# Recurrent block of a four-layer kernel: the h=1 scan level as a token-pair sum on VectorE, and four mixes at once on four row groups

## Chip, cores and metric

The kernel runs on one core of a Trainium2 chip. The metric is device time in microseconds (us), the median of three runs. All data are float32.

## What is computed

The input x is 32 sequences (B) of 128 tokens (T) with D = 512. Four layers follow each other: attention over a context (layer 0), a non-local block (layer 1), a recurrent block of the RWKV kind (layer 2), and cross-attention with a perceptron (layer 3). The change lies in layer 2. There NH = 32 heads of HD = 16 columns are scanned:

```
xa  = layer_norm(x);  sx = previous token of xa - xa
xxx = tanh((xa + sx * maa_x) @ maa_w1)             # five groups of 32 columns
xm_j = xa + sx * (maa_stack_j + xxx_j @ maa_w2_j)  # five mixes: k, w, v, r, g
w = exp(-exp(time_decay + tanh(xw @ td_w1) @ td_w2))
r, k, v = xr @ Wr.T, xk @ Wk.T, xv @ Wv.T;  g = silu(xg @ Wg.T)
for each token t:                                  # state s: 16 x 16 for each head
    a   = k_t (outer) v_t
    out = r_t . (u * a + s)
    s   = a + w_t * s
x1 = x + (group_norm(out) * g) @ Wo.T
x2 = x1 + sigmoid(xr2 @ Wfr.T) * (relu(xk2 @ Wfk.T)**2 @ Wfv.T)
```

## The kernel before

The program has stages: phase_a (layers 0 and 1), phase_norm, phase_b (layer 2) and phase_c (layer 3). phase_b begins at about 1050 us and ends at about 2900 us. It takes the sequences two at a time (G = 2), so there are N = 16 pairs, and a loop of turns (function `run`). The order of work is written out by hand. `SLOTS_OF` (L756) has 18 rows. In row n every engine does scan step n of the current pair and then the steps of the other stages that the row lists: kind "p" (projections of the next pair), "l" (late projections of the current pair), "f" and "e" (what follows the scan, for the pair before and the one before that). Each engine walks the same table in its own program; semaphores tie them. An engine does its own instructions strictly in this order, so an instruction that waits holds all behind it.

**The scan** has for each of the two sequences nine steps: seven levels h = 1, 2, 4, ..., 64, then PRODUCT and TURNED. At level h the tokens are cut into blocks of 2h, and TensorE makes the scores of the later h tokens against the earlier h (`scan` at L1297, matmuls at L1313: 16 for a level, on four row groups of 32 rows, one for each bank of the PSUM tensor `pS`). VectorE (h < 16) copies them by a mask into the score matrix `A` (L1626), ScalarE does it for h of 16 and more (L1473). GpSimd then multiplies the later columns of `R` (r split by head parity) and the earlier columns of `kT` by the decay totals (L1790, L1794), which the next level needs. The tensor `pS` is one buffer (banks=1), so that a score step waits until the step before has been drained. PRODUCT (L1321, L1326) multiplies `A` with the padded v (`v_pad`); ScalarE copies the result to `oT` (L1478) and splits R for the second sequence (L1463); TURNED transposes it (L1330). VectorE then forms in `o` the token's own term, v times `usum` = sum of r*u*k over a head (L1634), and adds the transposed product (L1640).

**The ring.** Results of all other matmuls go through `R_`, a ring of RING = 4 banks of PSUM (`pR`). The n-th item takes bank n mod 4, and `fill` waits until the item four before it was drained.

**The mixes.** Step h makes tanh's argument for the five mixes; ScalarE writes `hid` (L1406). The steps a0, a1 (mixes 0 and 1, halves 0 and 1) and b0, b1 (mixes 2 and 3) fill two banks each (L1251): a matmul has 32 rows, and the two mixes of a step lie on different row groups. VectorE drains a bank with two instructions (L1603), GpSimd adds xa (L1745) and raises `xm_ready`. The projections k, r, v, g wait for their mix. Steps named x and y are halves of one item. Step "gate" transposes `o` (L1217) into items gn0 and gn1, which ScalarE drains into `z` (L1497); o0 and o1 are the output projection (L1208).

The step "u" sums r*u*k over heads (L1290), "ut" transposes it (L1295). SyncE issues all DMAs.

Of the kernel before, what the change touches and what calls it, by code (L numbers as in the profile page):

```python
# [140 lines left out]
def phase_a(nc, dram, stats, kept):  # L141
# [34 lines left out]
    with ExitStack() as ctx:  # L176
# [3 lines left out]
        def sig(name, per):  # L180
            return Signal(ctx.enter_context(nc.semaphore("a_" + name)), per)
# [555 lines left out]
def phase_b(nc, dram, norm, kept):  # L737
# [9 lines left out]
    SLOTS = len(LEVELS) + 2  # L747
# [4 lines left out]
    PAIRS = {"a": ("m0", "m1"), "b": ("m2", "m3")}  # L752
# [72 lines left out]
    s_items = [(("s", g, k), "dve" if k == TURNED or k in SCORES and LEVELS[k] < RECT else "act") for g in range(G) for k in range(SLOTS)]  # L825

    with ExitStack() as ctx:
# [1494 lines left out]
```

## Time and profile before

| | |
|---|---|
| median of 3 runs | 4291.24 us (4286.19 to 4292.06) |
| the profiled execution: its own time, which is its span | 4293.0 us |
| TensorE busy | 4063.9 us, 95% |
| VectorE busy | 2301.4 us, 54% |
| ScalarE busy | 1503.0 us, 35% |
| GpSimd busy | 1419.2 us, 33% |

The page's busy time is a union of the instructions of an engine. A float32 matmul stands in the trace as two records, so 16 matmuls are "x32". Matmuls on different row groups run together, and their durations overlap. A number in square brackets behind a row is how long the engine was idle before it, and what ended that. PE is TensorE, PEld its weight loads, DVE VectorE, ACT ScalarE, POOL GpSimd.

### The profile page before, as it was taken

What the parts mean: (1) busy time and instruction counts of PE and PEld (TensorE: products, weight loads), DVE (VectorE), ACT (ScalarE), POOL (GpSimd) and SP (SyncE); (2) the same over time, 40 slices, a digit from 0 to 9 for tenths busy, and PEclk for the clock granted to TensorE, in tenths of its full rate; (3) what the DMA queues carried; (4) which work ended last, traced back from release to release, by engine and by line L of the source; (5) the groups of instructions that cost most, each with busy time, mean ns of one, the idle gap of its engine ahead of it and who ended that gap; (6) DMA issues with size and microseconds to landing.
All of it is one profiled execution on the core that took longest, in us unless ns stands there. A gap on an engine that the chain in (4) does not pass through costs nothing. (4 is left out here: it accounts for less than half of the span.)

```text
span 4293.0 us, 80239 instructions
## 1 busy us (share of the span) xinstructions
PE 4063.9 (95%) x31072; PEld 2552.2 (59%) x31072; DVE 2301.4 (54%) x2657; ACT 1503.0 (35%) x2622; POOL 1419.2 (33%) x1181
## 2 busy tenths in 40 slices
PE   6999999997999999999999999997999999999998
PEld 5666666664666666666666666654445545445443
DVE  3666666663367676666667766325434434434420
ACT  2555555553233344333343333211212222222220
POOL 2343333332254455544445544202211211211210
PEclk9999999998999999999999999998999999999999
DMA  3222222213210010000000001123010110110100
GB/s 109 70 78 65 77 70 77 78 51 106 98 70 26 27 37 26 27 26 27 26 26 26 29 29 62 72 76 149 10 40 0 40 40 0 41 40 0 41 10 10
DMA packets 121024, 205.22 MB, mean 48 GB/s; under 512 B 18784, under 2 KB 39264, under 8 KB 119200
## 3 DMA queue, kind: packets, MB, share of 16 engines
q1 hardware_dynamic: 120736, 200.80, 13.6%
q8 instruction: 251, 4.11, 0.4%
q14 instruction: 37, 0.30, 0.0%
HBM read 125.24 MB, written 67.11 MB: 45 GB/s over the span
## 5 line engine op out<-in xcount | busy, mean ns | idle before, releaser
L1626 DVE COPY_PREDICATED b_A<-b_mask,b_pS 128x2048 f32<-128x2048 uint32 x128 | 458.6, 3582 | 193.9 <-PE b_pS L1313 192.9
L2079 PE MATMUL c_pR<-c_proj_w,c_fcT 128*128 128x512 f32 x1024 | 460.0, 597 | 7.2 <-PEq L1926 3.2
L2019 PE MATMUL c_pR<-s_Wfr,c_fc_w 128*128 128x512 f32 x1024 | 458.4, 598 | 6.4 <-issue 2.3
L718 POOL TENSOR_TENSOR a_S<-a_S,a_negmax 128x2048 f32<-128x2048 f32 x64 | 231.1, 3611 | 489.8 <-DVE a_negmax L652 489.8
L1790 POOL TENSOR_TENSOR b_R<-b_R,b_Wh 128x512 f32<-128x512 f32 x192 | 228.1, 1188 | 394.1 <-PE b_pS L1313 393.8
L2019 PEld LDWEIGHTS c_pR<-s_Wfr,c_fc_w 128*128 128x128 f32 x1024 | 192.2, 191 | 245.5 <-issue 240.9
L2079 PEld LDWEIGHTS c_pR<-c_proj_w,c_fcT 128*128 128x128 f32 x1024 | 189.2, 190 | 235.3 <-issue 224.1
L1313 PE MATMUL b_pS<-b_R,b_kT 32*128 32x128 f32 x7168 | 265.3, 284 | 42.5 <-ACT b_A L1473 30.6
L1313 PEld LDWEIGHTS b_pS<-b_R,b_kT 32*128 32x128 f32 x7168 | 222.7, 186 | 137.8 <-issue 102.5
L2190 DVE TENSOR_TENSOR c_res<-c_res,c_pR 128x512 f32<-128x512 f32 x128 | 88.1, 688 | 402.2 <-PE c_pR L2079 377.3
L2089 ACT ACTIVATE c_fcT<-c_pR,s_vec 128x512 f32<-128x512 f32 x128 | 88.0, 688 | 609.5 <-PE c_pR L2019 580.7
L2216 POOL TENSOR_TENSOR c_S<-c_S,c_negmax 128x1024 f32<-128x1024 f32 x64 | 121.4, 1897 | 527.1 <-DVE c_negmax L2162 527.1
L1745 POOL TENSOR_TENSOR b_xm<-b_xm,b_xT 128x512 f32<-128x512 f32 x160 | 206.7, 1317 | 84.1 <-DVE b_xm L1603 83.8
L648 DVE SCALAR_TENSOR_TENSOR a_S<-a_pS,a_mask 128x2048 f32<-128x2048 f32 x64 | 146.3, 2285 | 143.1 <-PE a_pS L433 143.0
L1473 ACT ACTIVATE b_A<-b_pS 16x512 f32<-16x512 f32 (+2 forms) x224 | 199.3, 890 | 51.1 <-PE b_pS L1313 49.6
L566 ACT ACTIVATE a_probsT<-a_pR 128x512 f32<-128x512 f32 x256 | 138.6, 600 | 206.1 <-PE a_pR L442 205.6
L2170 DVE RECIPROCAL c_rec<-c_pR 128x256 f32<-128x256 f32 x64 | 112.5, 1757 | 158.2 <-PE c_pR L2064 153.9
L668 DVE RECIPROCAL a_rec<-a_pR 128x256 f32<-128x256 f32 x64 | 112.5, 1758 | 125.5 <-PE a_pR L457 120.6
L2201 POOL TENSOR_TENSOR c_rstd<-c_veps,c_half 128x1 f32<-128x1 f32 x64 | 41.1, 642 | 378.7 <-DVE c_veps L2129 378.7
L1790 POOL TENSOR_TENSOR b_R<-b_R,b_wT 128x512 f32<-128x512 f32 x32 | 48.3, 1509 | 333.1 <-PE b_pS L1313 333.1
L442 PEld LDWEIGHTS a_pR<-a_ident,a_S 128*128 128x128 f32 x1024 | 119.0, 146 | 59.8 <-issue 59.1
L1195 PE MATMUL b_pR<-b_xm,s_Wr 128*128 128x256 f32 x512 | 141.6, 439 | 8.4 <-POOL b_xm L1745 8.3
(257 smaller groups left out, 7911.6 us busy)
## 6 DMA issues: line engine op xcount, KB each, us to landing
a_c<-ctx SPq DMA_DIRECT2D x16, 512.0 KB, 4.0
a_x<-x SPq DMA_DIRECT2D x16, 512.0 KB, 5.0
a_kexp<-a_kT SPq DMA_DIRECT2D x512, 16.0 KB, 1.8
mid_cT<-a_cT SPq DMA_DIRECT2D x16, 512.0 KB, 2.7
a_xl<-x SPq DMA_DIRECT2D x32, 256.0 KB, 2.8
a_cl<-ctx SPq DMA_DIRECT2D x32, 256.0 KB, 3.0
mid_x<-a_xl SPq DMA_DIRECT2D x32, 256.0 KB, 3.3
mid_wy<-a_wy SPq DMA_DIRECT2D x32, 256.0 KB, 2.1
```

The lines of the kernel that those rows point to most:

```text
L566: nc.scalar.activation(probsT[n % 2][:, at:at + 4, :], bank.rearrange("p (h t) -> p h t", h=4), ACT.Exp).then_inc(*emptied["act"].up())
L648: nc.vector.scalar_tensor_tensor(out=S[n % 2][:, :, :], in0=pS[:, :, :].rearrange("p r (h t) -> p (r h) t", t=T), scalar=float(HD) ** -0.5 ...
L718: nc.gpsimd.tensor_tensor(S[n % 2][:, :, :], S[n % 2][:, :, :], negmax[n % 2][:, :].unsqueeze(2).to_broadcast([P, RH, T]), ALU.add)\
L1195: mm = nc.tensor.matmul(bank[:, m * TOK:m * TOK + TOK], w[:, c, at:at + P], src[:, c, :], start=(c == 0), stop=(c == KC - 1))
L1313: mm = nc.tensor.matmul(pS[:, r, c * P:c * P + P].rearrange("p (e n h) -> p e n h", e=2, h=h), kT[par][at, c, g * T:g * T + T], later, sta ...
L1473: ins = nc.scalar.activation(A[rows, :, 2 * h * b + h:2 * h * b + 2 * h], pS[rows, :, :].rearrange("p r (q t) -> p (r q) t", t=T // 2)[:, ...
L1626: nc.vector.copy_predicated(A[:, :, :].rearrange("p q (n two h) -> p q n two h", two=2, h=h)[:, :, :, 1, :], masks[h][:, :].bitcast(U32).r ...
L1745: nc.gpsimd.tensor_tensor(part, part, xT[0][:, 2 * h:2 * h + 2, :, 1:T + 1].rearrange("p k g t -> p (k g) t"), ALU.add)\
L1790: nc.gpsimd.tensor_tensor(later, later, decay, ALU.mult).then_inc(*r_moved.up())
L2019: mm = nc.tensor.matmul(bank, w[:, c, at * P:at * P + P], src[:, c, :], start=(c == 0), stop=(c == KC - 1))
L2079: mm = nc.tensor.matmul(bank, fcT[part % 2][:, m, g * T:g * T + T], proj_w[:, KC * part + m, :], start=(m == 0), stop=(m == KC - 1))
L2216: nc.gpsimd.tensor_tensor(S[n % 2][:, :, :], S[n % 2][:, :, :], negmax[n % 2][:, :].unsqueeze(2).to_broadcast([P, UH, T]), ALU.add)\
```

## The change

1. Level h = 1 has no scores any more (`SCORED = LEVELS[1:]`), so a sequence has eight scan steps and a turn 16. What the level gave, the term of an odd token from the token before it, is a sum over the head of r(odd) * k(even), times v of the even token. `rk1` holds the products, and step u makes the sums with four more matmuls (`heads_wide`, now 40 columns wide). `v_last` holds v moved on by one token; a DMA issued by ScalarE copies it from `v_pad` after each drain of v. VectorE multiplies it by the sums and adds it to `o` in TURNED.
2. R and kT are still multiplied by the h=1 decays. The first move of R for the first sequence, both moves of kT and the decay totals are now done by GpSimd in step "first", ahead of the scan; the move of R for the second sequence in PRODUCT.
3. The steps a0, a1, b0, b1 become a0 and a1. Each fills all four banks with mixes 0 to 3 of one half. GpSimd's sums of mixes 3 and 2 are steps of their own (sum3, sum2). There are four tiles for mixes in place of three.
4. The table has 16 rows. Step "gate" now stands ahead of a0 (it stood behind a1), g1y one row earlier than a0, td behind k0y.
5. `wT`, `v_pad` and `usum` have one buffer in place of two; `uT` and `hid` share one. Each has a wait for the last reader in the turn before. The semaphores of phase_a are cleared and freed.

```diff
-    SLOTS = len(LEVELS) + 2
+    SCORED = LEVELS[1:]
+    SLOTS = len(SCORED) + 2
     STEPS = G * SLOTS
     DM, DD = 32, 64
     LORA = ["k", "w", "v", "r", "g"]
 
-    PAIRS = {"a": ("m0", "m1"), "b": ("m2", "m3")}
+    MIXES = ("m0", "m1", "m2", "m3")
+    SUMMED = [("m0", 0), ("m1", 0), ("m0", 1), ("m1", 1), ("m3", 0), ("m3", 1), ("m2", 0), ("m2", 1), ("m4", 0), ("m4", 1)]
...
-        [("p", "h"), ("f", "gn_div")],
-        [("l", "g1y"), ("p", "a0")],
+        [("p", "h"), ("f", "gn_div"), ("l", "g1y")],
+        [("f", "gate"), ("p", "a0")],
         [("p", "a1")],
-        [("f", "gate"), ("p", "k0x")],
-        [("f", "o0"), ("p", "k0y")],
-        [("p", "td"), ("f", "o1")],
+        [("p", "k0x"), ("f", "o0")],
+        [("p", "k0y"), ("p", "td"), ("f", "o1")],
         [("p", "w"), ("f", "stats"), ("p", "k1x")],
-        [("p", "k1y"), ("f", "whiten"), ("p", "b0")],
-        [("p", "b0 sum"), ("f", "n2"), ("p", "b1")],
-        [("p", "m4"), ("f", "shift"), ("p", "r0")],
+        [("p", "k1y"), ("f", "whiten"), ("p", "sum3"), ("f", "n2")],
+        [("p", "m4"), ("f", "shift"), ("p", "r0"), ("p", "sum2")],
...
+        if name[0] == "a":
+            return [((m, int(name[1])), "dve") for m in MIXES]
...
-        xm = [sb("xm%d" % j, [P, KC, TOK]) for j in range(3)]
-        xm = [xm[0], xm[1], xm[0], xm[1], xm[2]]
-        hid = sb("hid", [P, TOK])
-        kT, wT, gT = (pair(n, [P, KC, TOK]) for n in ("kT", "wT", "gT"))
-        rT = sb("rT", [P, KC, TOK])
-        v_pad = pair("v_pad", [P, G, NH // 2, 3 * HD])
-        usum, s0 = pair("usum", [P, G, NH]), pair("s0", [P, KC, G, HD])
+        xm = [sb("xm%d" % j, [P, KC, TOK]) for j in range(4)]
+        xm = [xm[0], xm[1], xm[2], xm[3], xm[1]]
+        hid = uT = sb("hid", [P, TOK])
+        kT, gT = (pair(n, [P, KC, TOK]) for n in ("kT", "gT"))
+        rT, wT, rk1 = sb("rT", [P, KC, TOK]), sb("wT", [P, KC, TOK]), sb("rk1", [P, KC, TOK // 2])
+        v_pad, v_last = (sb(n, [P, G, NH // 2, 3 * HD]) for n in ("v_pad", "v_last"))
+        usum, s0 = sb("usum", [P, G, 2, NH]), pair("s0", [P, KC, G, HD])
...
+                elif s[0] == "a":
 
                     h = int(s[1])
-                    banks = [fill(pe, R_, pR, i, m, h, moved=[("h", 0)]) for m in PAIRS[s[0]]]
+                    banks = [fill(pe, R_, pR, i, m, h, moved=[("h", 0)]) for m in MIXES]
                     for m in range(2):
                         at = (2 * h + m) * P
-                        for name, bank in zip(PAIRS[s[0]], banks):
+                        for name, bank in zip(MIXES, banks):
...
+                        nc.tensor.matmul(bank[32 * c:32 * c + 32, 0:TOK], heads_wide[:, HC:], ruk[:, c, :], start=True, stop=False, skip_group_check=True)
+                    for c in range(KC):
+                        mm = nc.tensor.matmul(bank[32 * c:32 * c + 32, 0:TOK].rearrange("p (n two) -> p n two", two=2)[:, :, 1], heads_wide[:, 0:32], rk1[:, c, :],
+                                              start=False, stop=True, skip_group_check=True)
...
+                    h = SCORED[k]
+                    pe.wait_ge(*r_moved(i, g * len(LEVELS) + k + 1))
+                    pe.wait_ge(*k_moved(i, k_scaled(g, k + 1)))
...
+                        act.wait_ge(*r_moved(i + -1, len(LEVELS) + 1))
...
+                    act.wait_ge(*R_.out(i, "v", g))
+                    nc.scalar.dma_start(v_last[1:P:2, g, :, :].rearrange("p n z -> p (n z)"), v_pad[0:P:2, g, :, :].rearrange("p n z -> p (n z)")).then_inc(*v_moved[g].up(16))
...
+                elif s[0] == "a":
+                    h = int(s[1])
+                    if h == 0 and (i + -1).exists():
+                        dve.wait_ge(*R_.full(i + -1, "v", 1))
+                        dve.wait_ge(*R_.full(i + -1, "g", 1))
+                    for j, name in enumerate(MIXES):
...
+                    odd, even = (tile[:, :, :].rearrange("p c (n two) -> p c n two", two=2) for tile in (rT, kT[par]))
+                    nc.vector.tensor_tensor(rk1[:, :, :], odd[:, :, :, 1], even[:, :, :, 0], ALU.mult)
...
+                    own = o[:, g, :].rearrange("p (n e j) -> p n e j", e=2, j=HD)
+                    nc.vector.tensor_tensor(own, of_heads(v_pad), sums(0), ALU.mult).then_inc(*own_ready.up())
+                    dve.wait_ge(*v_moved[g](i, 16))
+                    nc.vector.tensor_tensor(of_heads(v_last), of_heads(v_last), sums(1), ALU.mult).then_inc(*last_ready.up())
                     dve.wait_ge(*own_ready(i, g + 1))
+                    dve.wait_ge(*last_ready(i, 2 * g + 1))
+                    nc.vector.tensor_tensor(own, own, of_heads(v_last), ALU.add).then_inc(*last_ready.up())
+                    dve.wait_ge(*last_ready(i, 2 * g + 2))
...
+                elif s in ("a0", "a1", "sum3", "sum2", "m4"):
+                    for name, h in {"a0": SUMMED[0:2], "a1": SUMMED[2:4], "sum3": SUMMED[4:6], "sum2": SUMMED[6:8], "m4": SUMMED[8:10]}[s]:
...
+                elif s == "first":
+                    pool.wait_ge(*decay_ready.all(i))
+                    pool.wait_ge(*ruk_ready(i, 1))
+                    pool.wait_ge(*r_split(i, 1))
+                    move_r(0, 1)
+                    for g in range(G):
+                        move_k(par, g, 1)
+                    pair_totals(i)
...
+            def move_r(g, h):
+                if h == 1:
+                    later = R[:, :, :, :].rearrange("p e c (n two) -> p e c n two", two=2)[:, :, :, :, 1]
+                    decay = totals(g, h)[:, :, :, 0].unsqueeze(1).to_broadcast([P, 2, KC, T // 2])
+                else:
+                    later = R[:, :, :, :].rearrange("p e c t -> p e (c t)").rearrange("p e (m two h) -> p e m two h", two=2, h=h)[:, :, :, 1, :]
+                    m = KC * T // (2 * h)
+                    decay = totals(g, h).rearrange("p c n two -> p (c n) two")[:, :, 0].unsqueeze(1).unsqueeze(3).to_broadcast([P, 2, m, h])
+                nc.gpsimd.tensor_tensor(later, later, decay, ALU.mult).then_inc(*r_moved.up())
+
+            def move_k(par, g, h):
+                sooner = kT[par][:, :, g * T:g * T + T].rearrange("p c (n two h) -> p c n two h", two=2, h=h)[:, :, :, 0, :]
+                decay = totals(g, h)[:, :, :, 1].unsqueeze(3).to_broadcast([P, KC, T // (2 * h), h])
+                nc.gpsimd.tensor_tensor(sooner, sooner, decay, ALU.mult).then_inc(*k_moved.up())
...
+                    pool.wait_ge(*r_split(i, g + 2))
+                    move_r(g + 1, 1)
                     pool.wait_ge(*S_.full(i, "s", g, k))
                     spread_state(i, par, g + 1)
```

## Rows read from the trace of the kernel before

**Rows 1.** The page's head and its part 1: busy us (share of the span) xinstructions.

```profile
span 4293.0 us, 80239 instructions
...
PE 4063.9 (95%) x31072; PEld 2552.2 (59%) x31072; DVE 2301.4 (54%) x2657; ACT 1503.0 (35%) x2622; POOL 1419.2 (33%) x1181
```

**Rows 2.** Timeline of TensorE, start of step h: start us, us, engine, line.

```profile
1269.36 1.99 PE L1235 MATMUL b_pR<-b_xn,b_w 128*128 128x256 f32 x8
...
2587.05 1.99 PE L1235 MATMUL b_pR<-b_xn,b_w 128*128 128x256 f32 x8
```

**Rows 3.** Windows of 100 us: busy by engine, then PEclk, DMA share, GB/s.

```profile
1500.00:1600.00 100.00, 94.77 (x932) 66.11 (x930) 71.21 (x85) 40.03 (x70) 50.71 (x50) 1.00 0.08 28
...
1600.00:1700.00 100.00, 94.67 (x927) 66.74 (x927) 69.24 (x85) 40.02 (x70) 50.93 (x50) 0.98 0.08 28
```

**Rows 4.** Waits of TensorE, 1500 to 1900.4 us: us, times, longest.

```profile
PE b_pS L1313 <- ACT b_A L1473: 8.8, 12, 1.0
...
PE b_pR L1195 <- POOL b_xm L1745: 5.3, 7, 0.8
...
PE b_pR L1259 <- ACT b_xT L1391: 3.4, 4, 0.9
...
PE b_pS L1313 <- DVE b_A L1626: 2.1, 4, 0.5
```

**Rows 5.** A window of 2 us, and the timeline of steps r0 and r1.

```profile
1618.00:1620.00 2.00, 2.00 (x7) 1.55 (x6) 1.97 (x2) 0.00 (x0) 2.00 (x2) 0.50 0.00 0
...
1616.62 5.40 PE L1195 MATMUL b_pR<-b_xm,s_Wr 128*128 128x256 f32 x16 [0.65 <-POOL b_xm L1745]
...
1623.06 3.72 PE L1195 MATMUL b_pR<-b_xm,s_Wr 128*128 128x256 f32 x16
```

**Rows 6.** Timeline of TensorE from step a1 to o0.

```profile
1684.27 1.13 PE L1251 MATMUL b_pR<-b_hid,b_w2a 32*128 32x256 f32 x8
...
1685.34 0.66 PE L1330 MATMUL b_pS<-s_ident,b_oT 128*128 128x128 f32 x4
...
1685.83 1.04 PE L1217 MATMUL b_pR<-s_ident,b_o 128*128 128x128 f32 x8
...
1687.70 1.99 PE L1195 MATMUL b_pR<-b_xm,s_Wk 128*128 128x256 f32 x8 [0.84 <-POOL b_xm L1745]
...
1689.62 1.19 PE L1313 MATMUL b_pS<-b_R,b_kT 32*128 32x128 f32 x32
...
1690.74 3.70 PE L1208 MATMUL b_pR<-b_wWo,b_z 128*128 128x512 f32 x8
...
1694.28 1.89 PE L1195 MATMUL b_pR<-b_xm,s_Wk 128*128 128x256 f32 x8
```

**Rows 7.** Groups by form, 1500 to 1900.4 us: busy us, mean ns, idle before.

```profile
L1634 DVE TENSOR_TENSOR b_o<-b_v_pad,b_usum 128x512 f32<-128x512 f32 x8 | 7.1, 892 | 0.0
...
L1640 DVE TENSOR_TENSOR b_o<-b_o,b_pS 128x512 f32<-128x512 f32 x8 | 5.5, 688 | 30.0 <-PE b_pS L1330 29.5
...
L1290 PE MATMUL b_pR<-b_xn,b_heads_wide 128*32 128x256 f32 x32 | 2.6, 391 | 0.0
```

**Rows 8.** Timeline of VectorE and GpSimd around the same steps.

```profile
1645.19 1.51 POOL L1790 TENSOR_TENSOR b_R<-b_R,b_wT 128x512 f32<-128x512 f32 x1 [19.10 <-PE b_pS L1313]
...
1681.80 1.66 DVE L1603 SCALAR_TENSOR_TENSOR b_xm<-b_pR,s_vec,b_sx 128x256 f32<-128x256 f32 x4
...
1682.75 2.32 POOL L1745 TENSOR_TENSOR b_xm<-b_xm,b_xT 128x512 f32<-128x512 f32 x2 [1.71 <-DVE b_xm L1603]
...
1687.02 1.10 DVE L1634 TENSOR_TENSOR b_o<-b_v_pad,b_usum 128x512 f32<-128x512 f32 x1
...
1691.00 4.79 DVE L1626 COPY_PREDICATED b_A<-b_mask,b_pS 128x2048 f32<-128x2048 uint32 x1 [0.69 <-PE b_pS L1313]
```

**Rows 9.** Timeline of ScalarE behind the product step.

```profile
1684.41 0.60 ACT L1478 ACTIVATE b_oT<-b_pS 128x512 f32<-128x512 f32 x1 [3.32 <-PE b_pS L1326]
...
1686.47 1.93 ACT L1497 ACTIVATE b_z<-b_pR,s_vec 128x256 f32<-128x256 f32 x4 [0.24 <-PE b_pR L1217]
```

More of the change, by code:

```diff
@@ L180, in sig @@
         def sig(name, per):
-            return Signal(ctx.enter_context(nc.semaphore("a_" + name)), per)
+            return Signal(nc.alloc_semaphore(name="a_" + name), per)
         def pair(name, shape):
@@ L779, in fills @@
         name = {"gate": "gn"}.get(step, step)
-        if step[-1] == "x" or step in ("b0 sum", "x2", "stats", "whiten", "shift", "uk", "first") or step[:3] == "gn_":
+        if step[-1] == "x" or step in ("sum3", "sum2", "x2", "stats", "whiten", "shift", "uk", "first") or step[:3] == "gn_":
             return []
-        if name[0] in PAIRS:
-            return [((m, int(name[1])), "dve") for m in PAIRS[name[0]]]
+        if name[0] == "a":
+            return [((m, int(name[1])), "dve") for m in MIXES]
         name = name.rstrip("y")
@@ L794, in phase_b @@
     lags = {item[0][0]: 1 - LAG[kind] for kind, step in table for item in fills(kind, step)}
-    SCORES, PRODUCT, TURNED = range(len(LEVELS)), len(LEVELS), len(LEVELS) + 1
+    SCORES, PRODUCT, TURNED = range(len(SCORED)), len(SCORED), len(SCORED) + 1
     EARLY, LATE = (-1, 0, 1), (N - 1, N)
@@ L824, in phase_b @@
     unit_at = {(turn, name): (side, n) for side in range(2) for n, (turn, name, who, unit) in enumerate(sides[side])}
-    s_items = [(("s", g, k), "dve" if k == TURNED or k in SCORES and LEVELS[k] < RECT else "act") for g in range(G) for k in range(SLOTS)]
+    s_items = [(("s", g, k), "dve" if k == TURNED or k in SCORES and SCORED[k] < RECT else "act") for g in range(G) for k in range(SLOTS)]
     with ExitStack() as ctx:
@@ L864, in phase_b @@
         Wh = sb("Wh", [P, G * KC * (T - 2)])
-        masks = {h: sb("mask%d" % h, [P, T // 2]) for h in LEVELS if h < RECT}
+        masks = {h: sb("mask%d" % h, [P, T // 2]) for h in SCORED if h < RECT}
         s0_wide, oT = sb("s0_wide", [P, KC, HC, HD]), sb("oT", [P, D])
@@ L900, in phase_b @@
         r_joined, s0_spread = sig("r_joined", G), sig("s0_spread", G)
-        own_ready = sig("own", G)
+        own_ready, last_ready, v_moved = sig("own", G), sig("last", 2 * G), [sig("v_moved%d" % g, 16) for g in range(G)]
         gn_centred, gn_squared, gn_var, gn_root, gn_ready = (sig("gn" + n, 1) for n in ("c", "s", "v", "r", "o"))
@@ L925, in phase_b @@
         kv_halves = [[W["Wfv"][:, :, 0:TOK], W["Wfv"][:, :, TOK:], W["Wo"][:, :, 0:TOK], W["Wo"][:, :, TOK:]],
-                     [quarter(kT[0]), quarter(wT[0]), quarter(x1g), quarter(wyg)]]
-        kv_slots = [[columns(tile, n) for tile in tiles for n in range(2)] for tiles in ((z, sx[1], xn[1]), (xm[1], sx[0], xT[0]))]
+                     [quarter(kT[0]), quarter(xm[0]), quarter(x1g), quarter(wyg)]]
+        kv_slots = [[columns(tile, n) for tile in tiles for n in range(2)] for tiles in ((z, sx[1], xn[1]), (xm[3], sx[0], xT[0]))]
         kv_weights = {kind: sig("kv_weights" + kind, 0) for kind in "KV"}
@@ L1221, in project @@
             def project(i, par, s):
-                if s == "b0 sum":
+                if s in ("sum3", "sum2"):
                     return
@@ L1395, in project @@
             def project(i, par, s):
-                if s[-1] == "x" or s == "b0 sum":
+                if s[-1] == "x" or s in ("sum3", "sum2"):
                     return
@@ L1404, in project @@
                 elif s == "h":
+                    if (i + -1).exists():
+                        act.wait_ge(*R_.full(i + -1, "ut", G - 1))
                     bank = take(act, R_, pR, i, "h", 0)
@@ L1528, in _ @@
             nc.vector.memset(A[:, :, :], 0.0).then_inc(*consts.up())
-            for tile in v_pad:
+            for tile in (v_pad, v_last):
                 nc.vector.memset(tile[:, :, :, :], 0.0).then_inc(*consts.up())
@@ L1568, in project @@
             def project(i, par, s):
-                if s[-1] == "x" or s == "b0 sum":
+                if s[-1] == "x" or s in ("sum3", "sum2"):
                     return
@@ L1621, in scan @@
                 g, k = divmod(n, SLOTS)
-                if k in SCORES and LEVELS[k] < RECT:
-                    h = LEVELS[k]
+                if k in SCORES and SCORED[k] < RECT:
+                    h = SCORED[k]
                     dve.wait_ge(*S_.full(i, "s", g, k))
@@ L2224, in phase_c, with phase_norm @@
         assert not wrong, wrong
-def phase_norm(nc, dram, stats, norm):
+def phase_norm(nc, dram, stats, norm, spent):
     with ExitStack() as ctx:
```

99 lines of the change are left out of this document (40 added, 59 removed).

## Prediction

> **What bounds the kernel now.** I read the page first [rows 1]. TensorE is busy 4063.9 of 4293.0 us, 95%. So another engine matters only where TensorE waits for it. The change lies in the recurrent block (L737 to L1813), which runs from about 1050 to 2900 us. I then looked at how long one turn of its loop takes. The first matmuls of step h start at 1269.36 us in one turn and at 2587.05 us 13 turns later [rows 2]: (2587.05 - 1269.36) / 13 = 101.36 us a turn. By windows [rows 3] TensorE works 94.7 to 94.8 of each 100 us. What it waits for stands in the waits of TensorE over 400 us, nearly four turns [rows 4]: 19.6 us in all, 4.9 us a turn. The reader is to see that no single wait is large: 2.2 us a turn for ScalarE's drains of the scores, 1.3 for GpSimd's sums of the mixes, 0.85 for ScalarE's xT, 0.5 for VectorE's predicated copy. They are 27 short stalls, the longest 1.0 us.
>
> There is one more loss. From 1618 to 1620 us the granted clock is 0.50 [rows 5], that is 1.2 GHz, after a run of short matmuls with waits between them (steps b1 and m4). Step r0 then takes 5.40 us, where r1, the same 16 records, takes 3.72 us: 1.7 us lost. The clock over the 100 us from 1500 is 1.00 [rows 3], so not every turn pays; I put the mean loss at 1.4 us a turn.
>
> **What the change takes off TensorE.** (1) The scores of h=1 go for both batch elements: 2 steps of 16 matmuls. A step takes 1690.74 - 1689.62 = 1.12 us from its start to the next work's start [rows 6]. 2 x 1.12 = 2.24 us a turn. (2) The four pair steps a0, a1, b0, b1 become two steps of four mixes. A pair step (a1) takes 1685.34 - 1684.27 = 1.07 us [rows 6]; it has two row groups at work. With four row groups at work the eight matmuls of a step stand in the same four time slots, if four groups run together as they do in the score steps, where 16 matmuls of 128 columns on four groups cost 1.12 us. I take 1.07 us for the new step, so 2.14 us saved; if they did not run together at all it would be nothing. (3) Step u gets four matmuls of half the columns. The four old ones have 2.6 us in four turns [rows 7], 0.65 a turn; half of that is +0.3 (between 0 and 0.65). Together -4.1 us a turn.
>
> **What it takes off the others, and where they get more.** VectorE loses two predicated copies of the costly kind, 4.79 us each [rows 8], 9.6 us a turn. It gains per batch element a product of v_last with the sums and an addition: the row of the same shape (L1634) has a mean of 0.89 us and L1640 has 0.69 [rows 7], so 1.6 us twice, plus rk1, bounded by the same two rows. On VectorE the balance is about -5.6 us a turn. Its time is worth nothing by itself; places count. GpSimd does the first moves of R and kT in step "first", where today it sits idle for 19.1 us before its first move [rows 8], so they cost nothing there; without that cover at least the 1.51 us of the move would stand in front of the first score. ScalarE issues two DMAs a turn, after each v. v_last isn't read before the transposed product, five scan steps later; I price the DMAs at nothing, and their worst case is among the rivals. wT, v_pad and usum become single: each new wait (for the scan of the turn before) is over many microseconds earlier. The freed semaphores and the different mask and memset count lie in the few us between the stages, nothing that I can price from a row; below 2 us either way.
>
> **The stretch where the four mixes meet the ring.** The ring of TensorE's results has four banks. The new a0 fills all four at once, so before its first matmul all four must have been drained; today a pair step needs two. And the step "gate", which was after a1, now stands directly ahead of a0: its two banks (gn) are drained by ScalarE. Count from the end P of the product step; in today's turn P is 1684.27 [rows 6].
>
> ScalarE's queue after P is: oT, the split of R, then the four z of gate. Today z ends at 1686.47 + 1.93 = 1688.40 [rows 9], P + 4.1, of which 0.2 was a wait for the transposes; the queue is the same in the new order, so z ends at about P + 3.95. TensorE has finished gate at P + 1.04 and holds a0 until P + 4.05: a stall of 3.0 us. a0 ends at P + 5.1.
>
> VectorE then has to drain four banks: four instructions take 1.66 us for two banks [rows 8], so 3.35 us for four, until P + 8.5. TensorE does the transposes (0.49) and stands at a1, which needs all four banks again: it starts at P + 8.6, a stall of 3.0 us. Behind these drains in VectorE's queue is not a1 but scan step TURNED: own 0.89, last 0.89, their sum 0.7 to 0.8, the addition from PSUM 0.69, and three waits on itself: about 3.5 us, until P + 12.1. TensorE's next score step writes the same pS, so it waits for that: a1 ends at P + 9.7, the score starts at P + 12.2, a stall of 2.5 us. Now k0x needs the sum of (m0,1): VectorE drains it until P + 13.0, GpSimd adds 1.2 to 1.3 us (two take 2.32 us in this place [rows 8]), so k0x starts at P + 14.4 and stalls 1.1 us. After the four banks of a1 (P + 15.4) VectorE copies the h=2 scores, 4.8 us, until P + 20.2. TensorE has done score, k0x and o0 (3.54, [rows 6]) at P + 19.8, and stalls 0.5 us. Sum of stalls in the stretch 3.0 + 3.0 + 2.5 + 1.1 + 0.5 = 10.1 us. Today the same stretch has 0.84 (k0x) and 0.53: 1.4 us. So +8.7 us a turn.
>
> That is why the relief of VectorE is worth little: 9.6 us went where VectorE waited for TensorE, and the path a0, TURNED, a1, h=2 copy is 15.1 us of VectorE in one piece beside 10.2 us of TensorE.
>
> The Trainium skill, page "TensorEngine Tiling (Array Packing)", section Performance Considerations, says that tiling makes TensorE faster but not the emptying of PSUM, which can become the limit after a 4x packing, and advises both ScalarE and VectorE for it; here VectorE alone empties the mixes. By the packing alone the sum would be -4.1 us a turn, by this rule the stretch is VectorE's; the trace can't decide it before the change, the rows above give the price.
>
> **Waits outside the stretch.** ScalarE's drains of the large scores (2.2 us a turn): with one score step fewer ahead, the h=16 drain stands beside n1 and g0x, and no longer behind the square of the group norm, and h=32 beside g0y and g1x, the longest of these slots. The steps b0 and b1 are gone from between n2 and m4, so m4 no longer needs the banks of n2 (0.86) and r0 waits less for the sums (0.65 [rows 5]). Of the 3.7 us a turn there (2.2 + 0.85 + 0.65) I keep 0.4, for a drain that comes a little late: -3.3 us. Between 0 and -3.7.
>
> **Clock.** Today the fall comes after the thin part around m4; that part becomes denser. The new thin part is P + 1 to P + 14, where TensorE works 3.7 of 13 us; it is thinner than the one before today's fall. I expect the fall there and none at r0. The slow time would hit k0x and o0, costing 1.7 us, of which 0.5 is inside the last stall: 1.2 against today's 1.4. So -0.2.
>
> **Sum.** -4.1 - 3.3 + 8.7 - 0.2 = +1.1 us a turn. 15 turns have both the scan and a new projection: +16. The last scan turn has no mixes and gains 2.2 to 3. The opening turn has mixes without scan and is half bound by loads: nothing. 4293.0 + 13 = 4306 us for the profiled execution. Its own time is the 4293.0 us, 1.8 us above the median of the three runs, 4291.24. Forecast 4304 us.
>
> **Rivals.** (A) Faster. TensorE stays the bound: the stretch costs less than counted, because the drains overlap. For: each term is a chain of small waits and my order is that of the text of the program; VectorE enters the stretch with 9.6 us less work. Against: the chain begins at ScalarE's oT, which can't be earlier than P. Were the stretch to stall 1.4 us as today, a turn would lose 7.6 us and the kernel 117: 4175 us. With half of it, 5 us, the turn loses 4 us: about 4230. The tipping point is 9.0 us of stall in the stretch; my 10.1 is just above it, so this rival is near. 30 in 100. (B) The same stretch within a microsecond of 9.0: no change, 4283 to 4300. 18 in 100. (C) Slower by the clock: the fall in the thin stretch and a second one at r0, or one that lasts longer, 1.7 to 3.4 us a turn, and contention of GpSimd with VectorE (L1634 has also taken 1.10 against 0.68 [rows 8]) adds 0.5: +2.2 to +3.9 a turn above forecast, 4340 to 4365. 13 in 100. The page "TensorE: Matmul & The Clock Gate" (the Trainium skill, section on why this matters) says that idle gaps between bursts give the clock back to half; [rows 5] agree in that the fall follows waits. (D) v_last comes late: the DMA would have to take over 20 us; 2 in 100, 4330 us. My forecast, slower by 0.2 to 1%: 37 in 100.
>
> 0.2% (9 us) is about what a measurement of this kernel can tell from no change. Faster 0.30, same 0.18, slower 0.52. The range reaches into A (half the stalls hidden) and into C: 4235 to 4350. The likeliest case's own range is 4300 to 4335.
>
> **What the profile after would show.** Waits of TensorE: L1251's successor waiting for ScalarE b_z about 3.0 us and for VectorE b_xm about 3.0 us a turn, the score step for VectorE b_o 2.5 us. No wait of m4 for b_xT. TensorE's share of the turn down to about 89%. The mix step with 16 records in about 1.1 us; if it takes 2.1, (2) is wrong. The low clock ahead of k0x and not at r0. The forecast is wrong if the two waits at a0 and a1 together are under 5 us, or if the turn is not 101.5 to 103.5 us.

## The result, and the profile after

| | before | after |
|---|---|---|
| median of 14 runs each, on the same chip | 4290.49 us | 4304.07 us |
| ratio after / before | | 1.004, 95% interval 1.0028 to 1.0053 |
| profiled execution | 4293.0 us | 4301.0 us |

The change makes the kernel 0.4% slower. The forecast was 4304 us. One run of after took 6276.68 us with a lower clock throughout; the ratio leaves it out.

The page's head and part 1 of after, which answer to [rows 1]:

```profile
span 4301.0 us, 78473 instructions
...
PE 4019.7 (93%) x30176; PEld 2517.0 (59%) x30176; DVE 2259.1 (53%) x2705; ACT 1500.4 (35%) x2622; POOL 1420.2 (33%) x1178
```

TensorE has 44 us less to do and the span is 8 us longer. The timeline gives the start of step h in the same two turns as [rows 2] (the line is L1239 here):

```profile
1267.92 1.99 PE L1239 MATMUL b_pR<-b_xn,b_w 128*128 128x256 f32 x8
...
2599.02 1.99 PE L1239 MATMUL b_pR<-b_xn,b_w 128*128 128x256 f32 x8
```

(2599.02 - 1267.92) / 13 = 102.39 us a turn, against 101.36: +1.03 us. Up to the first of these rows after is 1.4 us ahead, the 13 turns cost 13.4, and what follows takes 4.0 less (4301.0 - 2599.02 = 1702.0 against 4293.0 - 2587.05 = 1706.0). That makes the 8.0 us of the span.

A window over these turns, TensorE alone: length, busy, granted clock (PEclk), DMA share, GB/s. First before, then after.

```profile
1269.00:2587.00 1318.00, 1251.80 (x12106) 0.98 0.08 28
```

```profile
1269.00:2587.00 1318.00, 1211.47 (x11225) 0.94 0.09 31
```

Idle share times turn: 0.0502 x 101.36 = 5.1 us before, 0.0808 x 102.39 = 8.3 us after. So a turn has 3.2 us more waiting and only 2.2 us less work, although two score steps and two pair steps are gone. The clock column says why the work fell so little: 0.94 for 0.98. The waits of TensorE from 1500 to 1900.4 us, nearly four turns (us, times, longest):

```profile
PE b_pR L1255 <- ACT b_z L1509: 10.9, 4, 2.7
PE b_pR L1255 <- DVE b_xm L1617: 9.9, 4, 3.2
PE b_pR L1221 <- DVE b_xn L1562: 5.2, 4, 1.3
PE b_pS L1316 <- DVE b_o L1665: 3.5, 3, 1.8
PE b_pS L1316 <- ACT b_A L1485: 1.6, 8, 0.2
PE b_pR L1199 <- DVE b_z L1575: 0.6, 4, 0.2
```

Against [rows 4]: the waits of m4 and of the steps on GpSimd's sums are gone, ScalarE's drains of the scores fell from 2.2 to 0.4 us a turn, and in their place stand a0 waiting for ScalarE (2.7), a1 for VectorE (2.5) and the score step for VectorE (0.9). The stretch itself, by the timeline of TensorE, to be laid beside [rows 6]:

```profile
1677.64 1.99 PE L1239 MATMUL b_pR<-b_xn,b_w 128*128 128x256 f32 x8
...
1685.26 1.09 PE L1221 MATMUL b_pR<-s_ident,b_o 128*128 128x128 f32 x8
1689.09 2.09 PE L1255 MATMUL b_pR<-b_hid,b_w2a 32*128 32x256 f32 x16 [2.73 <-ACT b_z L1509]
1691.11 1.12 PE L1333 MATMUL b_pS<-s_ident,b_oT 128*128 128x128 f32 x4
1694.48 2.09 PE L1255 MATMUL b_pR<-b_hid,b_w2a 32*128 32x256 f32 x16 [2.25 <-DVE b_xm L1617]
1697.40 2.09 PE L1316 MATMUL b_pS<-b_R,b_kT 32*128 32x128 f32 x32 [0.83 <-DVE b_o L1665]
1699.42 3.21 PE L1199 MATMUL b_pR<-b_xm,s_Wk 128*128 128x256 f32 x8
1702.46 3.60 PE L1212 MATMUL b_pR<-b_wWo,b_z 128*128 128x512 f32 x8
1705.99 1.17 PE L1316 MATMUL b_pS<-b_R,b_kT 32*128 32x128 f32 x32
```

The row at 1685.26 is gate (P of the prediction). The waits sum to 2.73 + 2.25 + 0.83 = 5.8 us, and every step from a0 to k0x takes up to twice its time at full clock (in windows over a0, a1 and the score step the granted clock is 0.50, that is 1.2 GHz): the score step 2.09 for 1.17, k0x 3.21 for 1.99. The reader is to see that nearly half of what the forecast booked as idle time appears as slow work. From P to the score of h=4 pass 1705.99 - 1685.26 = 20.7 us; the prediction had 20.3. VectorE's copy of the h=2 scores, which the forecast had as the last thing before this score, is done earlier, at 1700.21 + 4.72 = 1704.93 us, 19.7 us after P:

```profile
1700.21 4.72 DVE L1642 COPY_PREDICATED b_A<-b_mask,b_pS 128x2048 f32<-128x2048 uint32 x1
```

### The profile page after: what moved, and what is told of

It reads as the page before. It is cut to its first block and busy times, and to the rows that moved or that the text cites. A ratio compares the mean times of both kernels' runs of the same rounds, so it can differ in the third digit from the quotient of the medians.

```text
span 4301.0 us, 78473 instructions
## 1 busy us (share of the span) xinstructions
PE 4019.7 (93%) x30176; PEld 2517.0 (59%) x30176; DVE 2259.1 (53%) x2705; ACT 1500.4 (35%) x2622; POOL 1420.2 (33%) x1178
## 5 line engine op out<-in xcount | busy, mean ns | idle before, releaser
L1642 DVE COPY_PREDICATED b_A<-b_mask,b_pS 128x2048 f32<-128x2048 uint32 x96 | 304.1, 3168 | 152.9 <-PE b_pS L1316 152.2
L1316 PEld LDWEIGHTS b_pS<-b_R,b_kT 32*128 32x128 f32 x6144 | 202.0, 196 | 118.5 <-issue 95.7
L1316 PE MATMUL b_pS<-b_R,b_kT 32*128 32x128 f32 x6144 | 239.5, 294 | 29.0 <-DVE b_o L1665 16.8
L1199 PE MATMUL b_pR<-b_xm,s_Wk 128*128 128x256 f32 x512 | 146.2, 435 | 2.8 <-POOL b_xm L1770 2.8
L652 DVE TENSOR_REDUCE a_negmax<-a_S 128x16 f32<-128x2048 f32 x64 | 146.3, 2286 | 2.2
```

What stands on the lines that cost most here:

```text
L652: nc.vector.tensor_reduce(negmax[n % 2][:, :], S[n % 2][:, :, :], AX.X, ALU.max, negate=True).then_inc(*max_found.up())
L1199: mm = nc.tensor.matmul(bank[:, m * TOK:m * TOK + TOK], w[:, c, at:at + P], src[:, c, :], start=(c == 0), stop=(c == KC - 1))
L1316: mm = nc.tensor.matmul(pS[:, r, c * P:c * P + P].rearrange("p (e n h) -> p e n h", e=2, h=h), kT[par][at, c, g * T:g * T + T], later, sta ...
L1642: nc.vector.copy_predicated(A[:, :, :].rearrange("p q (n two h) -> p q n two h", two=2, h=h)[:, :, :, 1, :], masks[h][:, :].bitcast(U32).r ...
```

## The experiments

All times are medians of chip runs, and each ratio is to the kernel before on the same chip, with its 95% interval. To compare turns I give two moments of the second sequence, counted in the timeline from the start of step h: S2, the start of its h=2 score step (1697.40 - 1677.64 = 19.8 us in after), and S4, that of its h=4 score step (28.35 us in after). A number without a range is that of the settled turns in the middle of the loop.

**1. The gate product one step later.** In after, a0 waits for ScalarE to drain gate's banks. Here gate stands ahead of a1.

```diff
-        [("f", "gate"), ("p", "a0")],
-        [("p", "a1")],
+        [("p", "a0")],
+        [("f", "gate"), ("p", "a1")],
```

> The changed kernel with step gate one row later, ahead of a1 in place of ahead of a0. Theory (the ring: a0 needs four banks, two of them are gate's, which ScalarE drains behind oT and the split of R): the 2.7 us wait at a0 goes, VectorE's chain starts that much earlier, and the clock may stay up; 3 to 4 us a turn less, about 50 us: 4245 to 4260 us. Rival 1 (VectorE's work is the bound of the stretch wherever gate stands): the wait only moves to a1 and to the score step, within 10 us of 4304. Rival 2 (four banks at once are the cost, gate's place is nothing): same as rival 1.

4296.26 us, ratio 1.003 (1.0019 to 1.004): a miss. S2 came 2.8 us earlier, at 16.9 us. S4 did not: 27.7 to 28.1 us in the first three turns, then 28.2 to 28.3, and the turn is still 102.4. The timeline of TensorE shows where the 2.8 us went:

```profile
1684.73 1.15 PE L1255 MATMUL b_pR<-b_hid,b_w2a 32*128 32x256 f32 x16 [1.24 <-ACT b_z L1509]
1689.28 2.09 PE L1316 MATMUL b_pS<-b_R,b_kT 32*128 32x128 f32 x32 [3.40 <-DVE b_o L1665]
1692.40 3.78 PE L1199 MATMUL b_pR<-b_xm,s_Wk 128*128 128x256 f32 x8 [1.03 <-POOL b_xm L1770]
1695.97 4.66 PE L1212 MATMUL b_pR<-b_wWo,b_z 128*128 128x512 f32 x8
```

A wait for GpSimd's sum came in ahead of k0x, which starts at 20.06 us after h, and k0x and o0 take 3.78 and 4.66 us for 1.99 and 3.60. Both could be the cause; experiments 8 and 9 part them.

**2 to 4. One part alone.** Run 2 is the changed kernel with the pair steps a0, a1, b0, b1 put back (the scan part alone). Run 3 is the kernel before with four mixes at once (the mixes alone). Run 4 is run 2 with the steps around a0 in another order. The diff shows the rows of the table only. What belongs to them (fills, drains, sums) goes with them, and run 3 also takes over the four tiles for mixes and the single `wT`.

```diff
 (2, 4, on after)
-        [("p", "k1y"), ("f", "whiten"), ("p", "sum3"), ("f", "n2")],
-        [("p", "m4"), ("f", "shift"), ("p", "r0"), ("p", "sum2")],
+        [("p", "k1y"), ("f", "whiten"), ("p", "b0")],
+        [("p", "b0 sum"), ("f", "n2"), ("p", "b1"), ("p", "m4"), ("f", "shift"), ("p", "r0")],
 (3, on before)
-    PAIRS = {"a": ("m0", "m1"), "b": ("m2", "m3")}
+    MIXES = ("m0", "m1", "m2", "m3")
 (4 and 5)
-        [("p", "h"), ("f", "gn_div"), ("l", "g1y")],
-        [("f", "gate"), ("p", "a0")],
+        [("l", "g1y"), ("p", "h"), ("f", "gn_div"), ("p", "a0")],
         [("p", "a1")],
-        [("p", "k0x"), ("f", "o0")],
-        [("p", "k0y"), ("p", "td"), ("f", "o1")],
+        [("f", "gate"), ("p", "k0x")],
+        [("f", "o0"), ("p", "k0y")],
+        [("p", "td"), ("f", "o1")],
```

> The changed kernel with the four pair steps of before (two row groups, two banks a step), b1 ahead of m4; the scan part and the place of gate as changed. Theory: the scan part alone is a gain of about 2 us of TensorE a turn, and a pair step doesn't wait for gate's banks, so the stretch has 3 to 4 us of waits in place of 5.8 plus the slow clock; TensorE does 2.1 us more and waits about 1 us at m4: a turn of 98.5 to 100 us, 4245 to 4265 us. Rival (four row groups are a gain that the scan part eats up, by VectorE's products in TURNED): slower than the changed kernel, 4320 to 4340 us.

> The kernel before with the mixes part alone: a0 and a1 with four mixes each, sums of mixes 3 and 2 as in the changed kernel, four tiles for mixes, one wT; seven score levels, and gate behind a1 as before. Theory: with the product step between a0 and a1 and gate behind both, the drains have cover; TensorE -2.1, waits at m4 and r0 -1.5, no low clock -1.4, new waits +1 to +2.5 us a turn: 4235 to 4262 us. Rival (four banks at once cost what they give, wherever they stand): 4285 to 4310 us.

> The scan part of the change alone: four pair steps as before, two banks each, and the steps in the order of before (a0, product, a1, transposes, gate, k0x), only g1y is ahead of h. Theory (the token-pair sum is a gain of 2 us a turn on TensorE, and what cost time in the changed kernel is where the mixes and gate stand): a turn of 99 to 101 us, 4240 to 4275 us. Rival (VectorE's three products in TURNED cost as much as the scores gave, wherever the mixes stand): 4290 to 4310 us.

4390.88 us, 1.0245 (1.0226 to 1.0264); 4332.07 us, 1.0111 (1.0094 to 1.0128); 4365.81 us, 1.0185 (1.0169 to 1.0202). Three misses, all on the same side: I had taken both parts for gains by themselves, spoilt only by their meeting. Both lose alone, as they were placed here. The waits of TensorE over 1500 to 1901 us, run 2, then run 3:

```profile
PE b_pS L1315 <- DVE b_o L1665: 25.0, 4, 6.5
PE b_pR L1262 <- ACT b_xT L1393: 9.1, 4, 2.3
```

```profile
PE b_pS L1313 <- POOL b_kT L1799: 7.1, 8, 1.5
PE b_pS L1313 <- ACT b_A L1476: 7.1, 8, 1.0
PE b_pR L1251 <- DVE b_gT L1617: 6.3, 4, 1.6
PE b_pR L1217 <- DVE b_xn L1553: 4.0, 4, 1.5
```

In run 2 the score step waits up to 6.5 us a turn for the VectorE chain of step TURNED, and m4 waits 2.3 us for xT. In run 3, a0 waits 1.6 us for VectorE to empty the bank of g1, and all waits come to 8.2 us a turn against 5.0. Run 4 has no wait for b_o any more and is 25 us better than run 2, but keeps that of m4 (9.1 us in 400, as above) and one for GpSimd's sums of 4.1 us a turn. Why the pair steps make m4 wait for xT in after's scan but only 0.85 us before, I didn't settle.

**5. The changed kernel with a0's cover.** The same edit of the order on after itself, with four mixes at once: a0, product step, a1, transposes, gate, k0x. The product step lies between a0 and a1, and gate no longer ahead of either.

> The changed kernel, four mixes at once, with the steps in that same order: a0 ahead of the product step, a1 behind it, gate behind the transposes. Theory (cover: the product step's 3 us cover the drain of a0's four banks, 3.3 us, and gate isn't in anyone's way): waits at a0 about 0.8, at a1 0.4, at the score 1.5 to 2.8 us, low clock shorter; a turn of 99.5 to 101 us, 4250 to 4285 us, and if it is below the run with pairs, four at once are a gain where they have cover. Rival (four banks at once cost what they give): 10 to 40 us above the run with pairs.

4272.21 us, ratio 0.9966 (0.9952 to 0.9981): faster than both, as expected, though by another way, for a0 and a1 wait 1.6 and 1.7 us (0.8 and 0.4 expected). The turn is 98.8 us, the granted clock over the 13 turns 0.99, S2 at 18.3, S4 at 24.8 us. Its timeline, k0x to the h=4 score:

```profile
1675.31 1.99 PE L1199 MATMUL b_pR<-b_xm,s_Wk 128*128 128x256 f32 x8 [0.91 <-DVE b_xm L1617]
1678.88 1.19 PE L1316 MATMUL b_pS<-b_R,b_kT 32*128 32x128 f32 x32 [1.57 <-DVE b_o L1665]
1679.99 3.70 PE L1212 MATMUL b_pR<-b_wWo,b_z 128*128 128x512 f32 x8
1683.53 1.89 PE L1199 MATMUL b_pR<-b_xm,s_Wk 128*128 128x256 f32 x8
1685.35 1.17 PE L1316 MATMUL b_pS<-b_R,b_kT 32*128 32x128 f32 x32
```

All at full clock. The waits of this stretch (1.6 at a0, 1.7 at a1, 0.4, 0.9, 1.6) sum to 6.1 us, no less than the 5.8 of the shown turn of after. So it isn't less waiting here that won the 3.6 us a turn.

**6 and 7. Moving the h=2 score both ways.** Is S4 set by VectorE's chain in TURNED? Run 6 does the products of the own and last terms of the first sequence, and their sum, at the product step (the diff shows its condition only); run 7 does the own product twice.

```diff
 (6)
-                elif k == TURNED:
+                elif k == TURNED or (k == PRODUCT and g == 0):
 (7)
+                    nc.vector.tensor_tensor(own, of_heads(v_pad), sums(0), ALU.mult).then_inc(*twice.up())
+                    dve.wait_ge(*twice(i, g + 1))
```

> The changed kernel with VectorE's three instructions of the token's own term and of v_last for the first sequence (0.68, 0.68, 0.69 us) done at the product step, where VectorE waits 3.9 us for ScalarE's z, in place of behind the drains of a0. Theory A (VectorE's chain is what TensorE waits for at the score step): the score step starts 0.8 us earlier, and with it all behind: 4290 to 4296 us. Theory B (an earlier start is eaten by the low clock, as with gate moved, where the h=2 score came 2.3 us earlier and the h=4 score at the same time): 4300 to 4308 us.

> The changed kernel with the product of the own term done twice, for both sequences: 0.68 us more on VectorE ahead of each transposed product. Theory A (VectorE's chain sets the score step): 0.7 to 0.8 us a turn, 10 to 13 us: 4314 to 4318 us. Theory B (the low clock's end sets the stretch): 4302 to 4308 us.

4301.45 us, 1.003 (1.002 to 1.0039), and 4306.7 us, 1.0043 (1.0028 to 1.0059). Both lie where theory B has them. S2 came at 18.3 to 19.5 us in run 6 and at 20.0 in run 7; S4 at 27.1 to 29.6 (28.2 to 28.4 once the turns have settled) and at 28.3. Over 3 us of S2 (with run 1) S4 and the settled turn do not follow. The one turn of run 6 whose k0x ran at full clock (2.02 us in place of 3.78) has S4 at 27.1 and lasts 101.2 us. Whatever sets S4 takes an earlier start away and forgives a later one.

**8. Filling with transposes.** On after, gate's transposes issued twice and those of the first sequence's TURNED four times.

```diff
-                    for c in range(KC):
-                        mm = nc.tensor.transpose(pS[:, 1, c * P:c * P + P], oT[:, c * T:c * T + T], ident[:, :])
+                    for _ in range(4 if g == 0 else 1):
+                        for c in range(KC):
+                            mm = nc.tensor.transpose(pS[:, 1, c * P:c * P + P], oT[:, c * T:c * T + T], ident[:, :])
```

> The changed kernel with TensorE's waits in the stretch filled: the transposes of gate are done twice, those of TURNED for the first sequence four times (same results, 24 more transposes a turn in places where TensorE waits for ScalarE and VectorE). Theory that the low clock costs 1 to 2 us a turn beside the waits: granted clock stays at 1.00 there, k0x takes 1.9 in place of 3.0 us, 4275 to 4290 us. Rival (transposes don't keep the clock up): the repeats run at 1.2 GHz, a1 comes about 1 us later, 4310 to 4330 us. Rival (the clock is hidden by VectorE's chain): 4300 to 4308 us.

4311.51 us, 1.0061 (1.0047 to 1.0075). The low clock left a0 and a1 (1.15 us each) and stayed at the score step and k0x (3.65 us), so S4 stayed at 28.3. It shifted the low clock and cured nothing. The time is in the range of the first rival, but not by its mechanism: a1 came half a microsecond earlier, not later (16.3 us after h for 16.8).

**9. Filling with real matmuls, in two doses.** Both stand on run 1 and only add work. The first repeats TURNED's transposes once and the first row half of a1 until it has six copies; the second has eight copies of it and issues the second sequence's h=2 score three times over.

```diff
 (first)
-                    for m in range(2):
+                    for m in [0, 1] if h == 0 else [0, 0, 0, 0, 0, 0, 1]:
 (second, besides two more zeros)
+                    for _ in range(3 if g == 1 and h == 2 else 1):
                     for c in range(KC):
                         for r in range(4):
```

> The changed kernel with the gate product ahead of a1 (as in the first experiment), with the turned transposes of the first sequence issued twice, and with a1's four product matmuls of the first row half issued six times over, which fills the 3.4 us that TensorE waited for the own-term product with real matmuls. It adds work and takes none away. Theory (the low clock eats what an earlier start wins): the granted clock of the stretch stays at 1.00, the score of the second sequence's h=2 step starts 17 to 18 us after h, k0x takes about 1.9 and o0 3.5 us, the h=4 score starts 25 to 26 us after h instead of 28.2, the turn is about 100 us, 4255 to 4275 us. Rival (something else than the clock holds the h=4 score at 28.2 us): the turn stays at 102.4 or longer, 4296 to 4310 us.

> The one before (gate ahead of a1, repeated transposes, repeated product matmuls of a1, now eight times) with the score of the second sequence's h=2 step issued three times over as well. That fills the 1.9 us that TensorE waited there for k0x's input, which VectorE and GpSimd have ready 20.06 us after h whatever the score does. Again it only adds work. Theory (the low clock holds the h=4 score): with no idle time left in the stretch the granted clock stays at 1.00, k0x starts 20.1 to 20.6 us after h and takes about 1.9 us, o0 takes 3.6, the h=4 score starts 25.6 to 26.6 us after h, the turn is 99.8 to 101 us, 4250 to 4280 us. Rival (something else than the clock holds it): the clock comes back to 1.00 and the score still starts at 28.2 us, 4290 to 4310 us. If the clock stays low at k0x, the run tells nothing between them.

The first: 4290.86 us, 1.0018 (1.0007 to 1.0029), turn 102.4, S4 28.2. Its expectation missed, for the clock did not come back where it mattered: the score took 1.19 us at full clock, then TensorE waited 1.94 us for GpSimd's sum and k0x ran at 1.2 GHz from 20.08 us after h. But the kernel did not begin like that. In its first full turn, h at 1264.23, k0x still ran at full clock, after the same wait:

```profile
1284.58 1.99 PE L1199 MATMUL b_pR<-b_xm,s_Wk 128*128 128x256 f32 x8 [2.05 <-POOL b_xm L1771]
...
1290.33 1.17 PE L1316 MATMUL b_pS<-b_R,b_kT 32*128 32x128 f32 x32 [0.32 <-DVE b_A L1643]
```

That is 20.35 us after h for k0x and 26.1 for S4. In this turn and the three behind it k0x starts 20.35, 20.1, 20.1 and 20.1 us after h and takes 1.99, 2.83, 3.78 and 3.78 us; S4 comes at 26.1, 27.1, 28.2 and 28.2, and the turns last 100.1, 101.2, 102.3 and 102.3 us. The same program with the same start of k0x thus has turns of 100 and of 102 us, by the clock of k0x and o0.

The second dose: 4273.52 us, 0.998 (0.9965 to 0.9995), turn 100.04, S4 25.9, a hit in each number. Its window of 100 us and its timeline:

```profile
1600.00:1700.00 100.00, 95.82 (x999) 1.00 0.09 32
```

```profile
1676.37 1.99 PE L1239 MATMUL b_pR<-b_xn,b_w 128*128 128x256 f32 x8
...
1688.77 4.17 PE L1255 MATMUL b_pR<-b_hid,b_w2a 32*128 32x256 f32 x72 [1.24 <-ACT b_z L1511]
1693.34 3.01 PE L1317 MATMUL b_pS<-b_R,b_kT 32*128 32x128 f32 x96 [0.40 <-DVE b_o L1667]
1696.49 1.99 PE L1199 MATMUL b_pR<-b_xm,s_Wk 128*128 128x256 f32 x8
1698.31 3.60 PE L1212 MATMUL b_pR<-b_wWo,b_z 128*128 128x512 f32 x8
1702.31 1.17 PE L1317 MATMUL b_pS<-b_R,b_kT 32*128 32x128 f32 x32 [0.40 <-DVE b_A L1644]
```

k0x starts at 1696.49 - 1676.37 = 20.12 us after h, the same as in run 1 (20.06) to 0.1 us, and from there S4 is 25.9 - 20.1 = 5.8 us away instead of 8.2. The only thing that changed between k0x and S4 is the clock (and 0.4 us of wait). S4 now waits 0.4 us for VectorE's copy of the h=2 scores, so that copy is the next limit. TensorE does 64 matmuls more a turn for nothing, and the kernel is faster than run 1, and than before by 0.2%.

**10. g1y a row earlier, on run 5.** To take a0's wait for g1's bank away.

```diff
-        [("p", "shift"), ("l", "g0y"), ("f", "gn_var"), ("l", "g1x")],
-        [("l", "g1y"), ("p", "h"), ("f", "gn_div"), ("p", "a0")],
+        [("p", "shift"), ("l", "g0y"), ("f", "gn_var"), ("l", "g1x"), ("l", "g1y")],
+        [("p", "h"), ("f", "gn_div"), ("p", "a0")],
```

> The best version so far (four mixes at once in the order a0, product, a1, transposes, gate) with the transposes and the gate product g1y issued one row earlier, behind g1x. In it a0 waits 1.7 us a turn for VectorE's b_gT, which frees the bank that a0 writes. Theory: that wait goes, and part of it comes back at a1, whose own wait for the masked halves (1.7 us) was partly covered by it: 0 to 0.7 us less a turn, 4262 to 4272 us. Rival: the whole 1.7 us moves to a1, no change, 4270 to 4280 us.

4263.96 us, 0.9955 (0.994 to 0.9971), on another chip than run 5; the two intervals overlap, so it isn't shown to be better. The time is in the expected range, but of the waits the account was wrong: a0 now waits 1.6 us for ScalarE's hid, a1 only 0.3, and k0x 1.9 for GpSimd. But this kernel holds a comparison that needs no edit. Two neighbouring turns, h at 1663.85 and at 1762.26:

```profile
1663.85 1.99 PE L1239 MATMUL b_pR<-b_xn,b_w 128*128 128x256 f32 x8
...
1682.09 1.26 PE L1316 MATMUL b_pS<-b_R,b_kT 32*128 32x128 f32 x32 [0.51 <-DVE b_o L1665]
1683.27 3.70 PE L1212 MATMUL b_pR<-b_wWo,b_z 128*128 128x512 f32 x8
...
1688.63 1.17 PE L1316 MATMUL b_pS<-b_R,b_kT 32*128 32x128 f32 x32
```

```profile
1762.26 1.99 PE L1239 MATMUL b_pR<-b_xn,b_w 128*128 128x256 f32 x8
...
1780.41 2.09 PE L1316 MATMUL b_pS<-b_R,b_kT 32*128 32x128 f32 x32 [1.16 <-DVE b_o L1665]
1782.43 4.79 PE L1212 MATMUL b_pR<-b_wWo,b_z 128*128 128x512 f32 x8
...
1788.88 1.17 PE L1316 MATMUL b_pS<-b_R,b_kT 32*128 32x128 f32 x32
```

The same steps, S2 at 18.2 us in both: S4 comes at 24.8 in the one and at 26.6 in the other, and the turns last 98.4 and 100.2 us. The waits are not quite equal, 0.51 and 1.16 us at the score step, because k0x took 3.27 and 2.62; they are over when the score starts. From there the 1.8 us are the price of a low clock at the score step and o0.

## Why the prediction was right, and where it was not

The sum was right: +1.1 us a turn forecast, +1.03 measured, 4304 us forecast and measured. Two terms behind it were off by some 2 us a turn in opposite directions, so that the sum came out to 0.1 us is luck.

- **Work taken off (2.24 + 2.14 - 0.3).** Right. The step with four mixes takes 1.15 us in run 1 at full clock, about as long as a pair step [rows 6], so the four row groups did run together. In after it often takes 2.09, which the prediction had named as the sign that this term is wrong; here it is the sign of the low clock, for in the turn that starts at 1780.11 both a0 and a1 of after take 1.15. The four new matmuls of step u take 0.33 us from start to start.
- **The stretch.** The order of waits was right (a0 for ScalarE, a1 for VectorE, the score for b_o) and so was its length from P, 20.7 us for 20.3. Its division was wrong. a0 and a1 came close, 2.7 and 2.5 for 3.0 and 3.0. The score step waited 0.9 for 2.5, and k0x and the h=4 score not at all for 1.1 and 0.5: 6.1 us a turn in place of 10.1. At the h=4 score even the limit was another: VectorE's copy was done at P + 19.7, half a microsecond ahead of the forecast, and TensorE itself, slowed, came at P + 20.7. TensorE's share of the turn, forecast at about 89%, is 91.9%. The first reason is VectorE's part in TURNED, which I had at the rate of a contended row; here four instructions of 0.68 to 0.69 us each stand between 1694.34 and 1697.16. The second is the next point.
- **The clock, the term that failed.** I wrote that the slow time would hit k0x and o0 for 1.2 us against 1.4 today. It begins at a0: in the turn shown a0, the transposes, a1, score and k0x take 0.94 + 0.46 + 0.94 + 0.92 + 1.22 = 4.5 us more than at full clock (1.15, 0.66, 1.15, 1.17, 1.99). The place was right otherwise: in the shown turns r0 takes 3.72 us where [rows 5] have 5.40. Slow matmuls filled the waits that I had booked as idle. Over the whole turn the two errors cancel: the waits rose by 3.2 us where I had 8.7 - 3.3 = 5.4, and TensorE's busy time fell by 2.2 where 4.1 were taken off, so that slow work rose by about 1.9 us where I had -0.2. The 1.4 us that I put on the slow work of before were low too: added up row by row over 13 turns it is about 1.7 us a turn before and 3.9 after.
- **Waits outside the stretch (-3.3).** The waits named did go: m4's and r0's are 0, ScalarE's drains 0.4 for 2.2. One came that I had not seen, n2 for VectorE's whitening, 1.3 us a turn. -1.9 instead of -3.3.
- **The ends.** The last turns and what surrounds them took 5.4 us less, 1.4 ahead of the 13 turns and 4.0 behind them, against my -3 plus two turns' +1.1 each.
- **The DMAs.** Right to be priced at nothing: v_last lands 2.1 us after its issue, and no wait names it. Rival D is out.

Rival A (faster) was right that the stretch costs less waiting than 9.0 us, its tipping point, and yet the kernel is slower: the point was worked out with the clock as before. The Trainium skill, page "TensorE: Matmul & The Clock Gate", section "HAM oscillation — how this bites in real kernels", reports a kernel whose clock swings between the two levels because TensorE waits (there for DMAs) between groups of matmuls. The rows of after and of the last fill agree, 0.94 with waits of 2.7 and 2.3 us ahead of a0 and a1, and 1.00 with the stretch filled. Run 5 shows that the sum of the waits doesn't decide it: 6.1 us of them in the stretch, the longest 1.7, and the clock at 1.00.

What is shown: with k0x starting at the same moment, the clock alone moves S4 by 2.4 us (runs 1 and 9) and by 2 us within one kernel (the first fill of run 9), and with the score starting at the same moment by 1.8 us within another (run 10). In after itself it is less. Its first full turn, h at 1267.92, has S2 at 19.8 us like the others, but k0x at full clock (1.99 us): there S4 comes at 27.6 in place of 28.35 us, and the turn lasts 101.6 in place of 102.5. More than about 1 us is not to be had behind S2, for VectorE's copy of the h=2 scores ends 27.3 us after h in every such turn. So of the loss in after the low clock behind S2 explains about 1 us a turn; that faster a0 and a1 would bring VectorE's part forward as well is only hinted at, by the turns in which both take 1.15 us (S2 19.3, S4 28.1).

Why the turns of after and of runs 1, 6, 7, 8 and the first of 9 all settle at 102.4 us is open. The first fill of run 9 shows only how: the slow part of its turn grows from turn to turn until the turn has that length.

What the change could be worth: in the order of run 5 it is worth 0.3%. Scan part and mixes each cost time alone (+1.8 to +2.4% and +1.1%); together in that order the turn falls from 105.8 (run 4) to 98.8 us.

## What to carry to other kernels

Removing matmuls from a stretch that already waits need not only turn them into idle time: here TensorE ran much of what remained at half clock, and an earlier start was eaten whole. So count a thin stretch twice, once for its waits and once for the steps behind it at half rate, and look at the granted clock before reading the waits, since slow work hides them. When a step takes all banks of a ring, move independent work between it and its twin, and the step whose banks drain slowly away from in front of it: the same instructions in that order won 0.75% over the changed kernel.

## What was not expected of the hardware

- More work, less time: 64 redundant matmuls a turn raised the granted clock over the turns from 0.95 to 1.00 and took 2.3 us off each turn (run 9). A smaller dose left the clock low behind the next wait, and repeated transposes only moved the low clock to the next steps (run 8).
- A VectorE product of 128x512 takes 0.68 us alone and up to 1.67 beside a GpSimd operation of the same shape. In the first fill of run 9 the pair of GpSimd sums grew too, 3.21 us for 2.31:

```profile
1682.41 3.21 POOL L1771 TENSOR_TENSOR b_xm<-b_xm,b_xT 128x512 f32<-128x512 f32 x2
```

```profile
1682.92 1.67 DVE L1660 TENSOR_TENSOR b_v_last<-b_v_last,b_usum 128x512 f32<-128x512 f32 x1
1684.62 1.55 DVE L1663 TENSOR_TENSOR b_o<-b_o,b_v_last 128x512 f32<-128x512 f32 x1
```

An instruction that starts earlier can thus run into a neighbour's time and end late: moved ahead in run 1, TURNED's four took 4.8 us on VectorE (1684.26 to 1689.03) instead of the 2.8 in after.
